# Transformer layer with dense MoE on Trainium2: causal-mask multiplies from GpSimd to VectorE, and the gate block from before attention to after it

## The chip, the cores and the metric

The kernel runs on the 8 NeuronCores of one Trainium2 chip (two dies of four cores). Every core runs the same program on its own batch element; nothing is exchanged between them. The metric is the device time in microseconds of the slowest core. The engines are named as in the profile: PE (TensorE matmul), PEld (its weight loads), DVE (VectorE), ACT (ScalarE), POOL (GpSimd), SP (SyncE, which here only issues DMAs).

## The reference

For each of 8 batch elements, x has 2048 rows of 1024 values.

```python
xn = layernorm(x)
x = x + attn(xn, w_qkv, w_out) + ffn(xn, w1, b1, w2, b2, wr, br)

def attn(x, w_qkv, w_out):            # 16 heads of 64, causal
    q, k, v = split(x @ w_qkv.T)
    scores = where(causal, (q @ k.T) / 8, -1e30)
    return (softmax(scores) @ v) @ w_out.T

def ffn(x, w1, b1, w2, b2, wr, br):   # 4 experts, hidden 4096, top 2
    topv, topi = top_k(x @ wr + br, 2)
    gates = softmax(topv)
    y = gelu(x @ w1[e] + b1[e]) @ w2[e] + b2[e]      # for every expert e
    c = gelu(b1[e]) @ w2[e] + b2[e]
    return sum over k of gates_k * (y[topi_k] - c[topi_k] + sum_e c[e])
```

## The kernel before

The program is written as blocks. Within a block each engine has its own list of instructions in the order of the Python code and meets the others only through semaphores; at the end of a block all engines meet at a barrier (the rows of the profile that name L43 or L47, as releaser `PEq L43`).

1. Block 1 and 2: constants (the causal mask tile `masks`, 128x2048 bf16, is made on POOL, L236), layer norm, transposes of the normalised x into `xn_fm`, router logits `lgt`, their top-2 mask `mask2`, and the projections to `q_fm`, `k_fm` and `v_ext`.
2. Block 3: SP issues eight DMA transposes of `w_out` (L565). Then comes the **gate block**, L569 to L599: 16 small exponentials on ACT (`exa`, L571), a multiply, 16 reductions, a reciprocal and 16 scalings on DVE that give `agate` (the gate of each row and expert, L575 to L585), and 16 PE transposes (L593) with a DVE copy each (L596) into `aem`. `agate` is first read by the feed-forward (L913, L918) and `aem` by its last bias matmuls (L1023). Then attention.
3. Block 4: the dense feed-forward, 16 slabs of weights (4 experts by 4 groups of 1024 hidden units) by 4 tiles of 512 rows: `emit_h` (L868, gelu L876) and `emit_y` (L899, accumulate L918).
4. Block 5: x, the attention result (through the DRAM buffer `attn_sc`) and the accumulator are added and stored.

**Attention.** The queries come in four quarters `qt` of 512 columns. Quarter qt has `npair` = 2(qt+1) steps p, each over two key blocks of 128. For each quarter a loop goes over eight head pairs (h0, h1), and within it over p. For each head and step: two score matmuls (`emit_pair`, L691 and L697, into the PSUM pair P45 or P67), one exponential of 128x1024 on ACT (L705) into `p_sb`, and two AV matmuls (`emit_av`, L726 and L733) into one of three PSUM slots. There is one `p_sb` for h0 and one for h1. The last two steps of every head cross the diagonal, and there `p_sb` is multiplied in place by `masks` (L713): 4 masks for each head pair, 4 x 32 = 128 in all. In quarter 0 every step is such a step; in quarter 3 two of eight are.

PE's order within a head pair is QK h0, QK h1, then for each p: AV h0, QK h0 of p+1, AV h1, QK h1 of p+1. A finished head is normalised late: DVE copies its row of sums (`rrow`, L647, `flush_stage1`, at the end of its head pair), then within the next head pair `flush_stage2` takes Ln and Exp on ACT (L655, L658), spreads the result with a one-row matmul (L664), copies it on DVE (`rbsb`, L668) and multiplies on DVE into `attn_cat` (L676), which frees the slot. The output projection of a quarter (`emit_opuser`, L760, L765, with a DVE copy L773 and a store L780) is interleaved into the first head pair of the next quarter; that of quarter 3 stands at the end of the block. In quarter 3 POOL also issues loads of feed-forward weights: w1 of slab 0 in two halves behind the second and fourth head pair (L819, L825), and w2 of slab 0 and both weights of slab 1 behind the last AV matmul (L616, L608).

The mask and what it hangs on, before:

```python
W("gpsimd", "SS", ve)
vm = I("gpsimd", "SG", lambda g, psb=psb, j=j: g.tensor_tensor(
    psb[:], psb[:], masks[:, j * 1024:(j + 1) * 1024], ALU.mult))
v_use[p] = vm
v_uses[p] = "SG"
```

Of the kernel before, what the change touches and what calls it, by code (L numbers as in the profile page):

```python
# [18 lines left out]
NTS = 16  # L19
# [30 lines left out]
def build_nc():  # L50
# [41 lines left out]
    lgt = at("lgt", [128, 64], F32, 2976)  # L92
# [80 lines left out]
    TRS = [P4, P5, P6, P7]  # L173
# [8 lines left out]
    def W(eng, s, v):  # L182
        if v > 0:
            P.emit(eng, lambda e, s=s, v=v: e.wait_ge(sem[s], v))  # L184

    def Wtr(eng, entry):
        if isinstance(entry, tuple):
            for k in range(0, len(entry), 2):
                W(eng, entry[k], entry[k + 1])
        else:  # L190
            W(eng, "SV", entry)

    def I(eng, s, fn, n=1):
# [175 lines left out]
    tr_idx = 0  # L369
    tr_evac = {}  # L370
# [55 lines left out]
    for q_ in range(4):  # L426
        for k_ in range(4):
            ts = q_ * 4 + k_
# [6 lines left out]
            if ts >= 2:  # L435
# [37 lines left out]
        trp = TRS[tr_idx % 4]  # L473
# [17 lines left out]
        for k_ in range(4):  # L491
            ts = q_ * 4 + k_
            trp = TRS[tr_idx % 4]
            W("tensor", "SV", v_lem)
            if tr_idx >= 4:
                Wtr("tensor", tr_evac[tr_idx - 4])
            v_t = I("tensor", "ST", lambda t, k_=k_, trp=trp: t.transpose(
                trp[0:128, 0:4], lgt_em[0:4, k_ * 128:(k_ + 1) * 128],
                ident[0:4, 0:4]))
# [66 lines left out]
            bass.AP(w_outT, fc * 128, [[8192, 128], [1024, 8], [1, 128]]),  # L566
            woutbf_h.ap()[fc * 128:(fc + 1) * 128, :]), 16)

    v_ex_last = 0  # L569
    for ts in range(NTS):  # L570
        v_ex_last = I("scalar", "SS", lambda s, ts=ts: s.activation(  # L571
            exa[:, ts * 4:(ts + 1) * 4], lgt[:, ts * 4:(ts + 1) * 4], AF.Exp,
            bias=nm1a[:, ts:ts + 1]))
    W("vector", "SS", v_ex_last)
    E("vector", lambda v: v.tensor_tensor(g2a[:], exa[:], mask2[:], ALU.mult))  # L575
    E("vector", lambda v: v.drain())
    for ts in range(NTS):
        E("vector", lambda v, ts=ts: v.tensor_reduce(
            Sa[:, ts:ts + 1], g2a[:, ts * 4:(ts + 1) * 4], AX.X, ALU.add))
    E("vector", lambda v: v.drain())  # L580
    E("vector", lambda v: v.reciprocal(rSa[:], Sa[:]))
    E("vector", lambda v: v.drain())
    v_ag = [0] * NTS
    for ts in range(NTS):
        v_ag[ts] = I("vector", "SV", lambda v, ts=ts: v.tensor_scalar_mul(  # L585
            agate[:, ts * 4:(ts + 1) * 4], g2a[:, ts * 4:(ts + 1) * 4],
            rSa[:, ts:ts + 1]))
    for ts in range(NTS):
        trp = TRS[tr_idx % 4]
        if tr_idx >= 4:  # L590
            Wtr("tensor", tr_evac[tr_idx - 4])
        W("tensor", "SV", v_ag[ts])
        v_t = I("tensor", "ST", lambda t, ts=ts, trp=trp: t.transpose(  # L593
            trp[0:4, 0:128], agate[:, ts * 4:(ts + 1) * 4], ident[:]))
        W("vector", "ST", v_t)
        v_ev = I("vector", "SV", lambda v, ts=ts, trp=trp: v.tensor_copy(  # L596
            aem[:, ts * 128:(ts + 1) * 128], trp[0:4, 0:128]))
        tr_evac[tr_idx] = v_ev
        tr_idx += 1  # L599

    w1g = [w1g0, w1g1]
    w2g = [w2g0, w2g1]
    h_sb = [h_sb0, h_sb1]
# [30 lines left out]
    sc_guard = [("SV", tr_evac[tr_idx - 1]), ("SV", tr_evac[tr_idx - 1])]  # L634
# [47 lines left out]
    def emit_pair(qt, head, p, npair, v_use, v_uses):  # L682
        bpar = head % 2
        pair = head // 2
        hr = (head % 2) * 64
        pb = PB[bpar]
        psb = p_sb[bpar]
        kb0 = 2 * p
        gs, gv = sc_guard[bpar]
        W("tensor", gs, gv)  # L690
        E("tensor", lambda t, kb0=kb0, pb=pb, hr=hr, pair=pair, qt=qt: t.matmul(  # L691
            pb[:, 0:512],
            k_fm[hr:hr + 64, pair * 2048 + kb0 * 128:pair * 2048 + (kb0 + 1) * 128],
            q_fm[hr:hr + 64, pair * 2048 + qt * 512:pair * 2048 + (qt + 1) * 512],
            start=True, stop=True))
# [12 lines left out]
        v_use[p] = ve
        v_uses[p] = "SS"
        if p >= npair - 2:  # L710
            j = p - (npair - 2)
            W("gpsimd", "SS", ve)
            vm = I("gpsimd", "SG", lambda g, psb=psb, j=j: g.tensor_tensor(  # L713
                psb[:], psb[:], masks[:, j * 1024:(j + 1) * 1024], ALU.mult))
            v_use[p] = vm
            v_uses[p] = "SG"

    def emit_av(qt, head, p, npair, v_use, v_uses, v_avp):
        bpar = head % 2
# [64 lines left out]
    for qt in range(4):  # L784
# [3 lines left out]
        for i_hp, hp in enumerate(hporder):  # L788
# [247 lines left out]
    v_ag = [0] * 4  # L1036
# [66 lines left out]
```

How the kernel before makes its waits and increments, by code:

```python
    def W(eng, s, v):  # L182
        if v > 0:
            P.emit(eng, lambda e, s=s, v=v: e.wait_ge(sem[s], v))
# [8 lines left out]
    def I(eng, s, fn, n=1):  # L193
        if n >= 16 and C[s] > 0:
            W(eng, s, C[s])
        C[s] += n
        v = C[s]
        P.emit(eng, lambda e, fn=fn, s=s, n=n: fn(e).then_inc(sem[s], n))
        return v
```

## Time and profile before

| what | value |
|---|---|
| median of the 2 runs shown | 3450.77 us (3350.36 and 3551.18) |
| the profiled execution's own time | 3365.17 us |
| its span on the slowest core | 3363.6 us (the eight cores: 3335.6 to 3363.6) |
| PE busy | 2832.9 us, 84% |
| DVE, ACT, POOL busy | 697.5, 863.9 and 305.3 us |
| attention, first score matmul to feed-forward's first matmul | 377.5 to 1361.0 us |

The span runs from the first to the last instruction of one core; what lies around it is 1.6 us here. A row of the timeline gives start, duration, engine, line, operation and, in brackets, how long the engine had been idle and what released it. The granted PE clock (PEclk) is a share of 2.4 GHz: 0.50 is 1.2 GHz.

### The profile page before, as it was taken

To read this page: it belongs to the slowest core of one execution; us is meant where nothing else is said; L and a number is where in the kernel's file an instruction comes from. 1 tells how busy PE (TensorE), PEld (TensorE's weight loads), DVE (VectorE), ACT (ScalarE), POOL (GpSimd) and SP (SyncE) were. 2 spreads that over 40 slices of the span, in tenths; PEclk is the share of its full clock that TensorE was granted. 3 is DMA by queue.
4 is the path that set the end of the run, shared out by engine and by line. 5 is a ranking of instruction groups with operands and counts; after the bars stand their busy time and mean duration, and the time that the engine had idled before them with its cause. 6 is when DMAs were issued, how large, how long until landed. Compare 5 with 4: busy or idle time off the path is not lost. (4 is left out here: it accounts for less than half of the span.)

```text
span 3363.6 us, 29884 instructions; the slowest of 8 cores (3335.6 to 3363.6 us)
## 1 busy us (share of the span) xinstructions
PE 2832.9 (84%) x10932; PEld 1085.4 (32%) x11124; DVE 697.5 (21%) x929; ACT 863.9 (26%) x1169; POOL 305.3 (9%) x189
## 2 busy tenths in 40 slices
PE   3679657667777876899999999999999999999970
PEld 1234201111111111344444444444444444444420
DVE  5441321111111001011111111111111111111224
ACT  2212244434444553211111111121111111111100
POOL 0000352322212221000000000000000000000000
PEclk9779656565555556899999999999999999999955
DMA  6710100000001004121331133023303330330017
GB/s 148 96 33 1 25 0 25 0 25 0 0 13 25 13 0 74 27 33 18 50 51 23 29 51 50 12 39 51 51 1 50 51 46 5 51 50 1 1 53 246
DMA packets 79709, 127.86 MB, mean 38 GB/s; under 512 B 36174, under 2 KB 36302, under 8 KB 79314
## 3 DMA queue, kind: packets, MB, share of 16 engines
q0 software_dynamic: 33616, 75.50, 15.1%
q1 hardware_dynamic: 45954, 50.44, 4.9%
q8 instruction: 96, 1.57, 0.2%
q14 instruction: 43, 0.35, 0.0%
HBM read 176.26 MB, written 25.17 MB: 60 GB/s over the span
## 5 line engine op out<-in xcount | busy, mean ns | idle before, releaser
L868 PE MATMUL P<-xn_fm,w1g 128*128 128x512 bf16 x4024 | 891.5, 380 | 32.0 <-PEq L43 27.4
L899 PE MATMUL P<-w2g,h_sb 128*128 128x512 bf16 x4001 | 889.3, 379 | 5.0
L876 ACT ACTIVATE h_sb<-P,b_sb 128x512 bf16<-128x512 f32 x512 | 351.9, 687 | 1445.2 <-PE P L868 1445.2
L918 DVE SCALAR_TENSOR_TENSOR accum<-P,agate,accum 128x1024 f32<-128x1024 f32 x240 | 308.2, 1284 | 1379.8 <-PE P L899 1379.8
L868 PEld LDWEIGHTS P<-xn_fm,w1g 128*128 128x128 bf16 x4096 | 400.0, 98 | 515.7 <-issue 37.4
L899 PEld LDWEIGHTS P<-w2g,h_sb 128*128 128x128 bf16 x4096 | 400.8, 98 | 483.2
L705 ACT ACTIVATE p_sb<-P,cneg 128x1024 bf16<-128x1024 f32 x320 | 353.2, 1114 | 488.8 <-PE P L697 488.5
L726 PE MATMUL P<-p_sb,v_ext 128*65 128x512 bf16 x320 | 192.1, 600 | 211.8 <-POOL p_sb L713 152.5
L713 POOL TENSOR_TENSOR p_sb<-p_sb,masks 128x1024 bf16<-128x1024 bf16 x128 | 268.8, 2117 | 896.2 <-ACT p_sb L705 896.0
L733 PE MATMUL P<-p_sb,v_ext 128*65 128x512 bf16 x320 | 195.6, 611 | 0.0
L726 PEld LDWEIGHTS P<-p_sb,v_ext 128*65 128x65 bf16 x320 | 41.2, 129 | 470.8 <-issue 469.5
L668 DVE COPY rbsb<-P 64x512 f32<-64x512 f32 x64 | 43.7, 683 | 669.2 <-PE P L664 668.9
L697 PE MATMUL P<-q_fm,k_fm 64*128 64x512 bf16 x320 | 176.5, 612 | 0.0
L691 PE MATMUL P<-q_fm,k_fm 64*128 64x512 bf16 x320 | 169.2, 586 | 7.2 <-DVE proj L773 6.5
L608 POOL DMA_DIRECT2D w1g<-w x15 | 13.2, 877 | 1640.2 <-PE P L941 1640.2
L285 PE MATMUL P<-xn_fm,wqkvT 128*128 128x512 bf16 x436 | 125.2, 432 | 23.9 <-DVE k_fm L304 18.9
L691 PEld LDWEIGHTS P<-q_fm,k_fm 64*128 64x128 bf16 x320 | 28.9, 99 | 209.6 <-issue 209.6
L446 PE MATMUL P<-ident,xnf 128*128 128x128 f32 x128 | 33.8, 404 | 57.8 <-ACT xnf L437 55.6
L664 PE MATMUL P<-rbr,ones_bf 1*64 1x512 bf16 x64 | 39.5, 616 | 45.0 <-ACT rbr L658 40.8
L285 PEld LDWEIGHTS P<-xn_fm,wqkvT 128*128 128x128 bf16 x448 | 47.8, 108 | 90.1 <-issue 77.1
L760 PE MATMUL P<-w_outT,attn_cat 128*128 128x512 bf16 x232 | 61.2, 419 | 11.2 <-ACT p_sb L705 7.9
L941 PE MATMUL P<-w2g,hfake 128*1 128x512 bf16 x256 | 57.8, 379 | 0.0
(113 smaller groups left out, 989.2 us busy)
## 6 DMA issues: line engine op xcount, KB each, us to landing
w2g<-w POOLq DMA_DIRECT2D x16, 2048.0 KB, 29.4
w1g<-w POOLq DMA_DIRECT2D x15, 2048.0 KB, 18.5
attn_sc<-proj SPq DMA_DIRECT2D x16, 512.0 KB, 2.6
xrg<-x SPq DMA_DIRECT2D x4, 2048.0 KB, 11.7
arg<-attn_sc SPq DMA_DIRECT2D x4, 2048.0 KB, 16.7
y<-outr SPq DMA_DIRECT2D x16, 512.0 KB, 2.6
xA<-x SPq DMA_DIRECT2D x3, 2048.0 KB, 38.2
wqkv_bf<-w_qkv POOLq DMA_DIRECT2D x3, 2048.0 KB, 24.4
```

The lines of the kernel that those rows point to most:

```text
L285: t.matmul(pt[:, off:off + 512], wqkvT[:, dc * 3072 + fc8 * 128:dc * 3072 + (fc8 + 1) * 128], xn_fm[:, dc * 2048 + tt * 512:dc * 2048 + (t ...
L691: E("tensor", lambda t, kb0=kb0, pb=pb, hr=hr, pair=pair, qt=qt: t.matmul(pb[:, 0:512], k_fm[hr:hr + 64, pair * 2048 + kb0 * 128:pair * 20 ...
L697: t.matmul(pb[:, 512:1024], k_fm[hr:hr + 64, pair * 2048 + (kb0 + 1) * 128:pair * 2048 + (kb0 + 2) * 128], q_fm[hr:hr + 64, pair * 2048 + ...
L705: ve = I("scalar", "SS", lambda s, pb=pb, psb=psb: s.activation(psb[:], pb[:, 0:1024], AF.Exp, bias=cneg8[:, 0:1]))
L713: vm = I("gpsimd", "SG", lambda g, psb=psb, j=j: g.tensor_tensor(psb[:], psb[:], masks[:, j * 1024:(j + 1) * 1024], ALU.mult))
L726: E("tensor", lambda t, p=p, head=head, psb=psb, sl=sl: t.matmul(sl[0:65, :], bass.AP(v_ext, 2 * p * VW + head * 65, [[NTS * VW, 128], [1, ...
L733: psb=psb, sl=sl, av_stop=av_stop: t.matmul(sl[0:65, :], bass.AP(v_ext, (2 * p + 1) * VW + head * 65, [[NTS * VW, 128], [1, 65]]), psb[:, ...
L760: t.matmul(pb[:, half * 512:(half + 1) * 512], ac[:, ec * 512 + ts4 * 128:ec * 512 + (ts4 + 1) * 128], w_outT[:, ec * 1024 + half * 512:ec ...
L868: t.matmul(PH67[par][:, 0:512], w1g[buf][:, dc * 1024 + hc * 128:dc * 1024 + (hc + 1) * 128], xn_fm[:, dc * 2048 + tt * 512:dc * 2048 + (t ...
L876: s.activation(h_sb[tt % 2][:, hc * 512:(hc + 1) * 512], PH67[par][:, 0:512], AF.Gelu, bias=b1_sb[:, e_ * 32 + g_ * 8 + hc:e_ * 32 + g_ * ...
L899: pt=pt, st=st, sp=sp: t.matmul(pt[:, half * 512:(half + 1) * 512], h_sb[tt % 2][:, hc * 512 + ts4 * 128:hc * 512 + (ts4 + 1) * 128], w2g[ ...
L918: v.scalar_tensor_tensor(accum[:, tsg * 1024:(tsg + 1) * 1024], pt[:, 0:1024], agate[:, tsg * 4 + e_:tsg * 4 + e_ + 1], accum[:, tsg * 102 ...
```

## The change

Two edits.

1. The mask multiply of `emit_pair` is issued on DVE in place of POOL, with the same operands, and signals DVE's semaphore SV, on which the AV matmul then waits.
2. The gate block is emitted after the whole attention loop, at the end of the same block. Before its transposes PE waits for the last two projection copies, which use the same PSUM tiles.

```diff
-    v_ex_last = 0
-    for ts in range(NTS):
-        v_ex_last = I("scalar", "SS", lambda s, ts=ts: s.activation(
...
@@ emit_pair
         if p >= npair - 2:
             j = p - (npair - 2)
-            W("gpsimd", "SS", ve)
-            vm = I("gpsimd", "SG", lambda g, psb=psb, j=j: g.tensor_tensor(
+            W("vector", "SS", ve)
+            vm = I("vector", "SV", lambda v, psb=psb, j=j: v.tensor_tensor(
                 psb[:], psb[:], masks[:, j * 1024:(j + 1) * 1024], ALU.mult))
             v_use[p] = vm
-            v_uses[p] = "SG"
+            v_uses[p] = "SV"
@@ after the loop over qt, ahead of P.brk()
+    v_ex_last = 0
+    for ts in range(NTS):
+        v_ex_last = I("scalar", "SS", lambda s, ts=ts: s.activation(
...
+    W("tensor", *sc_guard[0])
+    W("tensor", *sc_guard[1])
+    for ts in range(NTS):
+        trp = TRS[tr_idx % 4]
...
```

PE where attention's block begins, before: the last gate transposes, then the first score matmuls and the first AV, which waits for POOL's semaphore SG.

```order
L593 MATMUL P45<-ident_43,agate_76 4x128 [waits SV] x2
L593 MATMUL P67<-ident_43,agate_76 4x128 [waits SV] x2
L691 MATMUL P45<-q_fm_90,k_fm_91 128x512 [waits SV]
L697 MATMUL P45<-q_fm_90,k_fm_91 128x512
L691 MATMUL P67<-q_fm_90,k_fm_91 128x512 [waits SV]
L697 MATMUL P67<-q_fm_90,k_fm_91 128x512
L726 MATMUL P23<-p_sb0_118,v_ext_92 65x512 [waits SG]
L733 MATMUL P23<-p_sb0_118,v_ext_92 65x512
```

The same place after the change: the barrier, then the score matmuls at once, and the AV waits for DVE's semaphore SV.

```order
L47 UNCONDITIONAL_BRANCH [waits barrier_Pool_Activation_PE_DVE_SP_release]
L659 MATMUL P45<-q_fm_90,k_fm_91 128x512 [waits SV]
L665 MATMUL P45<-q_fm_90,k_fm_91 128x512
L659 MATMUL P67<-q_fm_90,k_fm_91 128x512 [waits SV]
L665 MATMUL P67<-q_fm_90,k_fm_91 128x512
L694 MATMUL P23<-p_sb0_118,v_ext_92 65x512 [waits SV]
L701 MATMUL P23<-p_sb0_118,v_ext_92 65x512
L659 MATMUL P45<-q_fm_90,k_fm_91 128x512 [waits SS]
L665 MATMUL P45<-q_fm_90,k_fm_91 128x512
```

The 16 transposes are gone from here, and nothing else stands between the barrier and the score matmuls.

DVE in quarter 0, before, from the end of the first head pair on (`rrow` are the copies of the sums, `rbsb` and `attn_cat` the late normalisation of the previous head pair):

```order
L647 COPY rrow0_120<-P23 1x512 [waits ST]
L647 COPY rrow1_121<-P23 1x512 [waits ST]
L668 COPY rbsb0_126<-P01 64x512 [waits ST]
L676 TENSOR_TENSOR attn_cat_116<-P23,rbsb0_126 64x512
L668 COPY rbsb1_127<-P01 64x512 [waits ST]
L676 TENSOR_TENSOR attn_cat_116<-P23,rbsb1_127 64x512
L647 COPY rrow0_120<-P01 1x512 [waits ST]
L647 COPY rrow1_121<-P23 1x512 [waits ST]
```

DVE at the same place after the change:

```order
L615 COPY rrow0_120<-P23 1x512 [waits ST]
L615 COPY rrow1_121<-P23 1x512 [waits ST]
L681 TENSOR_TENSOR p_sb0_118<-p_sb0_118,masks_78 128x1024 [waits SS]
L681 TENSOR_TENSOR p_sb1_119<-p_sb1_119,masks_78 128x1024 [waits SS]
L636 COPY rbsb0_126<-P01 64x512 [waits ST]
L644 TENSOR_TENSOR attn_cat_116<-P23,rbsb0_126 64x512
L681 TENSOR_TENSOR p_sb0_118<-p_sb0_118,masks_78 128x1024 [waits SS]
L681 TENSOR_TENSOR p_sb1_119<-p_sb1_119,masks_78 128x1024 [waits SS]
L636 COPY rbsb1_127<-P01 64x512 [waits ST]
L644 TENSOR_TENSOR attn_cat_116<-P23,rbsb1_127 64x512
L615 COPY rrow0_120<-P01 1x512 [waits ST]
L615 COPY rrow1_121<-P23 1x512 [waits ST]
```

The masks of a head pair's first step now stand behind the two `rrow` copies of the head pair before it, and those of its second step behind the normalisation of that pair's first head.

PE at the end of attention's block, before: the last projection matmuls, the barrier, the feed-forward's first matmuls.

```order
L760 MATMUL P67<-w_outT_84,attn_cat2_117 128x512 [waits SQW,SV]
L760 MATMUL P67<-w_outT_84,attn_cat2_117 128x512 x14
L765 MATMUL P67<-w_outT_84,attn_cat2_117 128x512
L43 UNCONDITIONAL_BRANCH
L47 UNCONDITIONAL_BRANCH [waits barrier_Pool_Activation_PE_DVE_SP_release]
L868 MATMUL P67<-xn_fm_83,w1g0_103 128x512 [waits SW0]
```

After the change:

```order
L728 MATMUL P67<-w_outT_84,attn_cat2_117 128x512 x14
L733 MATMUL P67<-w_outT_84,attn_cat2_117 128x512
L837 MATMUL P45<-ident_43,agate_76 4x128 [waits SV] x2
L837 MATMUL P67<-ident_43,agate_76 4x128 [waits SV] x2
L837 MATMUL P45<-ident_43,agate_76 4x128 [waits SV] x2
L837 MATMUL P67<-ident_43,agate_76 4x128 [waits SV] x2
L837 MATMUL P45<-ident_43,agate_76 4x128 [waits SV] x2
L837 MATMUL P67<-ident_43,agate_76 4x128 [waits SV] x2
L837 MATMUL P45<-ident_43,agate_76 4x128 [waits SV] x2
L837 MATMUL P67<-ident_43,agate_76 4x128 [waits SV] x2
L43 UNCONDITIONAL_BRANCH
L47 UNCONDITIONAL_BRANCH [waits barrier_Pool_Activation_PE_DVE_SP_release]
L870 MATMUL P67<-xn_fm_83,w1g0_103 128x512 [waits SW0]
```

The transposes now stand between the last projection matmul and the barrier; DVE's and ACT's gate instructions likewise stand last in their lists ahead of it.

## Rows read from the trace of the kernel before

**Rows 1.** Groups by line: name, shapes, xcount | busy us, mean ns | idle before, releaser.
```profile
L713 POOL TENSOR_TENSOR p_sb<-p_sb,masks 128x1024 bf16<-128x1024 bf16 x128 | 268.8, 2117 | 896.2 <-ACT p_sb L705 896.0
...
L726 PE MATMUL P<-p_sb,v_ext 128*65 128x512 bf16 x320 | 192.1, 600 | 211.8 <-POOL p_sb L713 152.5 <-DVE rrow L647 27.5 <-DVE attn_cat L676 22.3
```

**Rows 2.** Windows, steady unmasked attention: us, busy by engine, PEclk, DMA share, GB/s.
```profile
1280.00:1290.00 10.00, 10.00 (x22) 1.56 (x20) 0.00 (x0) 5.81 (x6) 0.00 (x0) 0.50 0.00 0
```

**Rows 3.** Timeline where attention's block starts: start us, us, engine, line, operation.
```profile
364.84 1.28 ACT L571 ACT_TABLE_LOAD   x1 [55.55 <-PEq L43]
...
366.13 3.11 ACT L571 ACTIVATE exa<-lgt,nm1a 128x4 f32<-128x4 f32 x16
...
377.51 0.71 PE L691 MATMUL P<-q_fm,k_fm 64*128 64x512 bf16 x2 [0.53 <-DVE aem L596]
...
378.61 2.12 ACT L705 ACTIVATE p_sb<-P,cneg 128x1024 bf16<-128x1024 f32 x2 [9.37 <-PE P L697]
```

**Rows 4.** Groups by line: table load behind a wait; two VectorE tensor_tensor forms.
```profile
L676 DVE TENSOR_TENSOR attn_cat<-P,rbsb 64x512 bf16<-64x512 f32 x64 | 43.8, 684 | 8.5 <-issue 5.0 <-PE P L697 0.5
...
L392 DVE TENSOR_TENSOR xsq<-xA 128x1024 f32<-128x1024 f32 x16 | 19.6, 1225 | 7.6 <-DMA xA<-x 6.4
...
L413 ACT ACT_TABLE_LOAD x1 | 1.3, 1283 | 16.2 <-DVE var_a L410 16.2
```

**Rows 5.** Timeline, one head pair of query quarter 3, from score matmul to score matmul.
```profile
1190.84 0.61 PE L691 MATMUL P<-q_fm,k_fm 64*128 64x512 bf16 x2
...
1218.94 4.19 POOL L713 TENSOR_TENSOR p_sb<-p_sb,masks 128x1024 bf16<-128x1024 bf16 x2 [29.78 <-ACT p_sb L705]
...
1221.20 0.61 PE L726 MATMUL P<-p_sb,v_ext 128*65 128x512 bf16 x1 [1.72 <-POOL p_sb L713]
...
1223.28 0.60 PE L726 MATMUL P<-p_sb,v_ext 128*65 128x512 bf16 x1
...
1226.87 0.61 PE L726 MATMUL P<-p_sb,v_ext 128*65 128x512 bf16 x1 [1.60 <-POOL p_sb L713]
...
1228.94 0.60 PE L726 MATMUL P<-p_sb,v_ext 128*65 128x512 bf16 x1 [1.04 <-POOL p_sb L713]
...
1230.47 0.61 PE L691 MATMUL P<-q_fm,k_fm 64*128 64x512 bf16 x2
```

**Rows 6.** Timeline, one head pair of query quarter 0.
```profile
406.06 0.61 PE L691 MATMUL P<-q_fm,k_fm 64*128 64x512 bf16 x2
...
407.24 2.12 ACT L705 ACTIVATE p_sb<-P,cneg 128x1024 bf16<-128x1024 f32 x2 [3.81 <-PE P L697]
407.72 1.29 DVE L647 COPY rrow<-P 1x512 f32<-1x512 f32 x2
...
410.86 0.61 PE L726 MATMUL P<-p_sb,v_ext 128*65 128x512 bf16 x1 [3.77 <-POOL p_sb L713]
...
414.17 0.61 PE L726 MATMUL P<-p_sb,v_ext 128*65 128x512 bf16 x1 [0.75 <-DVE attn_cat L676]
...
417.09 0.61 PE L726 MATMUL P<-p_sb,v_ext 128*65 128x512 bf16 x1 [0.93 <-POOL p_sb L713]
...
419.84 0.61 PE L726 MATMUL P<-p_sb,v_ext 128*65 128x512 bf16 x1 [1.71 <-POOL p_sb L713]
...
421.36 0.61 PE L691 MATMUL P<-q_fm,k_fm 64*128 64x512 bf16 x2
```

**Rows 7.** Timeline, first head pair of quarter 1, where the output projection is interleaved.
```profile
531.28 0.38 PE L726 MATMUL P<-p_sb,v_ext 128*65 128x512 bf16 x1 [0.31 <-POOL p_sb L713]
```

**Rows 8.** Timeline from the last attention load issue to the feed-forward's first matmul.
```profile
1310.17 0.95 POOL L616 DMA_DIRECT2D w2g<-w  x1 [1.72 <-PE P L733]
...
1337.11 1.22 DVE L773 COPY proj<-P 128x1024 f32<-128x1024 f32 x1 [1.81 <-DMA attn_sc<-proj]
...
1361.00 29.99 PE L868 MATMUL P<-xn_fm,w1g 128*128 128x512 bf16 x126 [27.39 <-PEq L43]
```

**Rows 9.** Windows just before the feed-forward starts.
```profile
1355.00:1360.00 5.00, 0.00 (x0) 0.00 (x0) 0.00 (x0) 0.00 (x0) 0.00 (x0) 0.50 0.96 167
```

More of the change, by code:

```diff
@@ L567, in build_nc @@
             woutbf_h.ap()[fc * 128:(fc + 1) * 128, :]), 16)
-    v_ex_last = 0
-    for ts in range(NTS):
-        v_ex_last = I("scalar", "SS", lambda s, ts=ts: s.activation(
[L572 to L599, printed above, removed]
     w1g = [w1g0, w1g1]
@@ L841, in build_nc @@
             op_defer = []
+    v_ex_last = 0
+    for ts in range(NTS):
+        v_ex_last = I("scalar", "SS", lambda s, ts=ts: s.activation(
+            exa[:, ts * 4:(ts + 1) * 4], lgt[:, ts * 4:(ts + 1) * 4], AF.Exp,
+            bias=nm1a[:, ts:ts + 1]))
+    W("vector", "SS", v_ex_last)
+    E("vector", lambda v: v.tensor_tensor(g2a[:], exa[:], mask2[:], ALU.mult))
+    E("vector", lambda v: v.drain())
+    for ts in range(NTS):
+        E("vector", lambda v, ts=ts: v.tensor_reduce(
+            Sa[:, ts:ts + 1], g2a[:, ts * 4:(ts + 1) * 4], AX.X, ALU.add))
+    E("vector", lambda v: v.drain())
+    E("vector", lambda v: v.reciprocal(rSa[:], Sa[:]))
+    E("vector", lambda v: v.drain())
+    v_ag = [0] * NTS
+    for ts in range(NTS):
+        v_ag[ts] = I("vector", "SV", lambda v, ts=ts: v.tensor_scalar_mul(
+            agate[:, ts * 4:(ts + 1) * 4], g2a[:, ts * 4:(ts + 1) * 4],
+            rSa[:, ts:ts + 1]))
+    W("tensor", *sc_guard[0])
+    W("tensor", *sc_guard[1])
+    for ts in range(NTS):
+        trp = TRS[tr_idx % 4]
+        if tr_idx >= 4:
+            Wtr("tensor", tr_evac[tr_idx - 4])
+        W("tensor", "SV", v_ag[ts])
+        v_t = I("tensor", "ST", lambda t, ts=ts, trp=trp: t.transpose(
+            trp[0:4, 0:128], agate[:, ts * 4:(ts + 1) * 4], ident[:]))
+        W("vector", "ST", v_t)
+        v_ev = I("vector", "SV", lambda v, ts=ts, trp=trp: v.tensor_copy(
+            aem[:, ts * 128:(ts + 1) * 128], trp[0:4, 0:128]))
+        tr_evac[tr_idx] = v_ev
+        tr_idx += 1
     P.brk()
```

## The prediction, made before the changed kernel ran

> **What bounds the kernel now.** I read the groups by line first, for what PE waits for. The AV matmul L726 sat idle 211.8 us, 152.5 of them until POOL's mask L713 had ended; the mask takes 2117 ns and runs 128 times [rows 1]. The windows show that between masks PE is the bound: from 1280 to 1290 us it is busy 10.00 of 10 us, ACT 5.81, and the granted clock is 0.50, 1.2 GHz [rows 2]. So attention is PE's time plus its waits, and of the waits the masks make up the most. The timeline at the block's start gives the other part that the change touches: between the barrier (364.84) and the first score matmul (377.51) PE has nothing but the gate block [rows 3]. Last I read the block's end, since that is where the gate block goes: DVE's last copy ends at 1338.3 and PE starts the feed-forward only at 1361.0, after 27.39 us of idle time at the barrier, while the DMA engines are 0.96 busy until 1360 [rows 8, 9].
>
> **Edit 2, the start.** The first score matmul moves from 377.51 to about the barrier's 364.84, 12.7 us earlier. One thing is given back. ACT's table load of 1.28 us ran beside the barrier ahead of the gate's exponentials; now the first instruction on ACT is attention's exponential, which waits for the scores. The load at L413 started only when the wait of its instruction had ended [rows 4], so I take the whole 1.28 us as uncovered (the other bound is 0). That leaves 11.4 us (11.4 to 12.7). The eight w_out transposes on SP are issued at the barrier in either kernel and are first needed far later.
>
> **Edit 2, the end.** ACT, long idle by then, has its 16 exponentials (3.11 us) done before DVE's last copy ends. From the end of those exponentials to the first score matmul the gate chain took 377.51 - 369.24 = 8.3 us [rows 3], so it ends near 1338.3 + 8.3 = 1346.6, counted in times of before. What the feed-forward waits for is the barrier, and I read the barrier as waiting for the three weight loads whose issue begins on POOL at 1310.17, right behind the last AV matmul: the DMA engines go quiet at 1360, and PE starts 1 us later. From issue to PE's start that is 50.8 us, a stretch that moves as a whole with the last AV matmul. The gate chain lies inside it with 14 us to spare: cost 0 (bounds 0 and 8.3 plus some issue, if the cover is not there).
>
> **Edit 1, what a mask costs on DVE.** No row shows a bf16 multiply from SBUF on DVE. The rows on either side are 684 ns for a tensor_tensor of 512 f32 columns and 1225 ns for one of 1024 f32 columns [rows 4]. By columns the mask would be like the second, by bytes per partition like the first, since 1024 bf16 are as many bytes as 512 f32. I take 0.69 us, by bytes, and keep 1.225 as a rival.
>
> The Trainium skill (VectorE: DVE Perf Modes, the perf-mode tier table) says that tensor_tensor on packed bf16 operands in SBUF yields two results a cycle where f32 yields one, and its walkthrough gives 1224 ns for 2048 columns; an estimate from its fixed part of some 150 cycles is 690 ns for 1024. No row here shows the rule for bf16; its f32 half agrees with the 1225 ns. By it the sum below stands; without it the sum would be that of the first rival.
>
> **A head pair of quarters 1 to 3.** It takes 1230.47 - 1190.84 = 39.6 us in quarter 3 [rows 5]. Four AV matmuls follow masks. (a) The first comes at 1221.20 after 1.72 us of waiting; its mask began at 1218.94. On DVE that mask ends at 1219.63 and, with the 0.14 us that POOL's end took to reach PE (1218.94 + 2.12 to 1221.20), PE goes on at 1219.77: a wait of 0.3 remains, 1.43 saved. (b) The second comes at 1223.28, 0.15 after POOL's two masks end (1218.94 + 4.19); four matmuls from 1221.20 on keep PE until 1223.1 (22 take 10 us [rows 2], a little more where AV and score matmuls alternate), so 0.15 is saved. (c) The third waits 1.60 and keeps 0.3: 1.30 saved. (d) The fourth waits 1.04. Its scores are issued just before the third AV: 1.18 us from first score matmul to exponential (406.06 to 407.24 [rows 6]), 1.11 for it, 0.15 to the mask, 0.69 for the mask and 0.14 back make 3.27 us, against 1.93 us of matmuls and the 0.3 of (c). So 1.04 remains and nothing is saved: here the wait for the mask turns into one for the exponential. Sum 2.87 us for a head pair. In these quarters DVE's other work lies at the start of a head pair (normalisation) and behind its last AV (sum copies), so no other instruction stands in front of a mask for long.
>
> There are 24 such head pairs. In the first of quarter 1 the output projection lies between the masks and the AV that need them (one wait of 0.31 is left there [rows 7]), so I count nothing for it, and half for the first of quarter 2: 22.5 x 2.87 = 64.6 us.
>
> **A head pair of quarter 0.** It takes 421.36 - 406.06 = 15.3 us [rows 6]. The first exponential ends at 407.24 + 1.11 = 408.35, but DVE is at the two sum copies until 409.01, and the mask now stands behind them: it runs from 409.05 to 409.75, and the AV comes at 409.9 in place of 410.86, 0.95 saved. The second AV (414.17) waits for attn_cat, not for a mask, and moves along. The third loses its wait of 0.93 whole, for the mask starts beside the scores of the other head. The fourth waits 1.71 now and, by (d)'s chain with no wait in (c)'s place, keeps 3.27 - 1.93 = 1.34: 0.37 saved. Sum 2.25 us, times 8 = 18.0 us. Queued behind a waiting mask on DVE stand the next rbsb copy and the multiply into attn_cat; both wait for a matmul that PE issues later than the masked scores, so they lose nothing.
>
> **Sum.** 11.4 + 64.6 + 18.0 = 94.0 us. The profiled execution took 3365.2 us by its own time (span 3363.6): 3365.2 - 94.0 = 3271. The median shown for before, 3450.8, is of two runs 200 us apart; the lower of them, 3350.4, lies 15 us under the profiled time and would give 3256.
>
> **Rivals.**
> *The mask runs at the f32 rate, 1.225 us.* Waits (a) and (c) keep 0.84 each in place of 0.30, (b) still goes and (d) stays, so 1.79 us is saved for a head pair, 22.5 x 1.79 = 40.3. In quarter 0 the first wait saves 0.42 (0.95 less 0.53), the third still about 0.9 and the fourth loses 0.16: 1.2 x 8 = 9.6. With 11.4 that is 61.3: 3304. For it: the only 1024-column row is 1225 ns. Against: half the bytes.
> *The end has no cover.* If the barrier's 22 us after DVE's last copy were its own and not the loads', the gate chain would add its 8.3 us: 3280. Against: the DMA engines' 0.96 right up to 1360 [rows 9].
> *The clock rises.* With the stalls gone PE might be granted 1.0 in attention. ACT would then bound the steps at 5.81 of 10 us [rows 2]. 160 steps less the 64 masked ones are 96, of 8 matmuls each and about 3.6 us (22 matmuls in 10 us): 349 x 0.42 = 147 us more, 3124. Against: the window has PE busy throughout and the clock is 0.50 all the same.
> The Trainium skill (TensorE: Matmul & The Clock Gate, What's actually happening) has activity release the full clock and idleness take it back. By that rule alone this rival would win; the trace disagrees, with 0.50 at 10.00 us busy in 10.
> *Slower: DVE's masks become slower than POOL's.* DVE, unlike POOL, also has copies in its list, and one engine holding both could make a mask's turn effectively 2.45 us, twice the f32 row. Then waits (a), (b) and (c) each grow by 2.45 - 2.12 = 0.33, 1.0 us a head pair; in quarter 0, with 0.55 to 0.8 behind the sum copies, about 1.8. 22.5 + 14.4 - 11.4 = 25.5 us slower, 3391. It decides from about 2.2 us a mask on, and from 2.9 us the kernel is over 2% slower. For it: the two sum copies in front of quarter 0's masks. Against: both VectorE rows are far below, and in the later quarters no copy stands in front of a mask.
> *The change does not do what it says*, the wait only moving to the exponential: that is so for (d), and is in the sum.
>
> **How the numbers follow.** Forecast 0.76, f32 rate 0.12, no cover 0.06, clock 0.02, slower 0.04. About 2% is what a measurement of this kernel can tell from no change, 67 us, so below 3298. The forecast, the uncovered end and the clock are faster, but of the forecast I set 0.05 aside for gains that turn out a third smaller; of the f32-rate case, which lies on the line, a quarter counts as faster: 0.71 + 0.06 + 0.02 + 0.03 = 0.82. Within 2%: 0.05 + 0.09 + a quarter of the slower case, 0.15 in all after rounding; slower by over 2%, the rest: 0.03. The range goes from 3235 (the lower run of before less 94 is 3256, and less 21 for a mask shorter than any row and for errors of my chain) to 3330 (the f32 rate, 3304, with an uncovered end 8.3 more, and the 15 us between the two low times on top). It leaves out the clock and the slower case.
>
> **What would show it.** In the profile after: L681 on DVE, 128 times at about 0.69 us; PE's wait for it near 0.3 us for the first and third masked AV and 1.0 for the fourth, 50 to 70 us in all against 152.5; a head pair of quarter 3 at 36.7 us and one of quarter 0 at 13.0; the first score matmul right behind the barrier; the gate chain ended more than 10 us before the feed-forward's first matmul, which still comes some 51 us after POOL's L584 issue. The prediction is wrong if a mask takes over 1.1 us, if the head pairs keep their 39.6 us because another wait fills in, or if the barrier moves with the gate chain.

## The result, and the profile after

| | before | after |
|---|---|---|
| ratio, after to before, with its 95% interval | | 0.9708 (0.9668 to 0.9747) |
| profiled execution's own time | 3365.17 us | 3266.81 us |
| median of all executions | 3637.33 us (10) | 3361.26 us (11) |
| lowest execution | 3350.36 us | 3261.92 us |

The two medians hold executions in which one die was granted a lower clock, and can't be compared; the ratio is of undisturbed executions alone. It means 2.9% faster, 98 us of 3365. The prediction had 94 us (3271 of 3365, 0.972). Its range of 3235 to 3330 us holds the profiled execution and misses the median of all eleven, 3361.26. A twelfth execution of the kernel after, 3245.37 us, is on record and not counted in that median.

Where the time went, from the first and last starts of four lines (the V projection L324; the first score matmul of a step, L691 before and L659 after; the AV matmul L726 before and L694 after; the feed-forward's L868 before and L870 after), each the median over the eight cores:

| stretch | before, us | after, us |
|---|---|---|
| end of V projection to first score matmul | 14.1 | 1.6 |
| first score matmul to last AV | 933.1 | 840.8 |
| last AV to feed-forward's first matmul | 51.1 | 51.4 |
| feed-forward, first to last start of L868 / L870 | 1797.2 | 1797.4 |

So 12.5 us go at the start and 92.3 us in attention, only 0.3 us comes back at the end, and the feed-forward is untouched: 104.5 us on a typical core.

The groups by line of the kernel after, to set beside [rows 1]:

```profile
L694 PE MATMUL P<-p_sb,v_ext 128*65 128x512 bf16 x320 | 191.1, 597 | 124.1 <-DVE p_sb L681 66.3 <-DVE rrow L615 26.0 <-DVE attn_cat L644 22.2
...
L681 DVE TENSOR_TENSOR p_sb<-p_sb,masks 128x1024 bf16<-128x1024 bf16 x128 | 88.0, 691 | 408.2 <-ACT p_sb L673 408.2
```

The mask takes 691 ns on DVE in place of 2117 ns on POOL, and PE's wait for it fell from 152.5 to 66.3 us. The waits for `rrow` and `attn_cat` are what they were (27.5 and 22.3 before).

The timeline of a head pair's masked end in quarter 3, beside [rows 5]:

```profile
1061.22 0.69 DVE L681 TENSOR_TENSOR p_sb<-p_sb,masks 128x1024 bf16<-128x1024 bf16 x1 [21.10 <-ACT p_sb L673]
...
1062.06 0.61 PE L694 MATMUL P<-p_sb,v_ext 128*65 128x512 bf16 x1 [0.26 <-DVE p_sb L681]
...
1064.01 0.61 PE L694 MATMUL P<-p_sb,v_ext 128*65 128x512 bf16 x1
...
1066.27 0.61 PE L694 MATMUL P<-p_sb,v_ext 128*65 128x512 bf16 x1 [0.25 <-DVE p_sb L681]
...
1067.38 0.69 DVE L681 TENSOR_TENSOR p_sb<-p_sb,masks 128x1024 bf16<-128x1024 bf16 x1 [1.26 <-ACT p_sb L673]
...
1068.22 0.61 PE L694 MATMUL P<-p_sb,v_ext 128*65 128x512 bf16 x1 [0.92 <-DVE p_sb L681]
...
1069.75 0.61 PE L659 MATMUL P<-q_fm,k_fm 64*128 64x512 bf16 x2
```

The first masked AV waits 0.26 us (1.72 before), the second nothing, the third 0.25 (1.60), the fourth 0.92 (1.04). DVE had been idle 21.10 us ahead of the first mask.

The timeline of a head pair of quarter 0, beside [rows 6]:

```profile
396.76 0.61 PE L659 MATMUL P<-q_fm,k_fm 64*128 64x512 bf16 x2
...
398.43 1.29 DVE L615 COPY rrow<-P 1x512 f32<-1x512 f32 x2
399.65 1.27 DVE L681 TENSOR_TENSOR p_sb<-p_sb,masks 128x1024 bf16<-128x1024 bf16 x2
...
400.57 0.61 PE L694 MATMUL P<-p_sb,v_ext 128*65 128x512 bf16 x1 [2.77 <-DVE p_sb L681]
...
403.88 0.61 PE L694 MATMUL P<-p_sb,v_ext 128*65 128x512 bf16 x1 [0.75 <-DVE attn_cat L644]
...
405.80 0.64 PE L694 MATMUL P<-p_sb,v_ext 128*65 128x512 bf16 x1
...
408.08 0.60 PE L694 MATMUL P<-p_sb,v_ext 128*65 128x512 bf16 x1 [1.21 <-DVE p_sb L681]
...
409.61 0.61 PE L659 MATMUL P<-q_fm,k_fm 64*128 64x512 bf16 x2
```

The first mask starts at 399.65, where DVE's two sum copies end (398.43 + 1.29 = 399.72, within 0.07 us); the AV follows at 400.57. Score matmul to score matmul it is 12.85 us (15.3 before).

The timeline where attention's block begins, beside [rows 3]:

```profile
372.84 0.50 PE L659 MATMUL P<-q_fm,k_fm 64*128 64x512 bf16 x2 [1.27 <-PEq L43]
...
373.51 1.28 ACT L673 ACT_TABLE_LOAD   x1 [64.58 <-PE P L665]
374.80 2.12 ACT L673 ACTIVATE p_sb<-P,cneg 128x1024 bf16<-128x1024 f32 x2
```

Scores run right behind the barrier. The table load came after the scores, as taken from L413, with its whole 1.28 us; the exponential follows it at once. But the scores were shorter: the load starts 0.67 us behind the first score matmul, where the exponential of before started after 1.10 us. The granted clock was still 1.00 here (from 372.8 to 374.0 us) and 0.50 at the same place before. So the first exponential starts 1.96 us behind the first score matmul (1.10 before), and 0.86 us is given back.

The timeline at the block's end, beside [rows 8]:

```profile
1216.51 0.88 POOL L584 DMA_DIRECT2D w2g<-w  x1 [145.31 <-PE P L701]
...
1221.61 3.10 ACT L813 ACTIVATE exa<-lgt,nm1a 128x4 f32<-128x4 f32 x16
...
1243.37 1.22 DVE L741 COPY proj<-P 128x1024 f32<-128x1024 f32 x1 [1.53 <-DMA attn_sc<-proj]
1244.51 0.22 DVE L817 TENSOR_TENSOR g2a<-exa,mask 128x64 f32<-128x64 f32 x1
...
1249.58 3.10 DVE L840 COPY aem<-P 4x128 f32<-4x128 f32 x12 [0.29 <-PE P L837]
...
1266.49 18.75 PE L870 MATMUL P<-xn_fm,w1g 128*128 128x512 bf16 x74 [14.19 <-PEq L43]
```

The gate chain ends at 1252.7 (1249.58 + 3.10), 13.8 us ahead of the feed-forward, which starts 50.0 us behind the issue of the first of POOL's three loads (50.8 before).

### The profile page after: what moved, and what is told of

Read it like the earlier page. It is cut to its first block and busy times, and to the rows that moved or that the text cites. A ratio compares the mean times of both kernels' runs of the same rounds, so it can differ in the third digit from the quotient of the medians.

```text
span 3265.3 us, 30078 instructions; the slowest of 8 cores (3230.9 to 3265.3 us)
## 1 busy us (share of the span) xinstructions
PE 2852.7 (87%) x11124; PEld 1088.2 (33%) x11124; DVE 784.8 (24%) x1057; ACT 863.5 (26%) x1169; POOL 36.2 (1%) x61
## 3 DMA queue, kind: packets, MB, share of 16 engines
q0 software_dynamic: 33616, 75.50, 14.9%
## 5 line engine op out<-in xcount | busy, mean ns | idle before, releaser
L870 PE MATMUL P<-xn_fm,w1g 128*128 128x512 bf16 x4096 | 897.1, 380 | 14.2 <-PEq L43 14.2
L870 PEld LDWEIGHTS P<-xn_fm,w1g 128*128 128x128 bf16 x4096 | 400.1, 98 | 502.5 <-issue 24.6
L694 PE MATMUL P<-p_sb,v_ext 128*65 128x512 bf16 x320 | 191.1, 597 | 124.1 <-DVE p_sb L681 66.3
L681 DVE TENSOR_TENSOR p_sb<-p_sb,masks 128x1024 bf16<-128x1024 bf16 x128 | 88.0, 691 | 408.2 <-ACT p_sb L673 408.2
L659 PE MATMUL P<-q_fm,k_fm 64*128 64x512 bf16 x320 | 168.3, 582 | 7.9 <-DVE proj L741 6.5
L694 PEld LDWEIGHTS P<-p_sb,v_ext 128*65 128x65 bf16 x320 | 41.0, 128 | 379.0 <-issue 377.6
L659 PEld LDWEIGHTS P<-q_fm,k_fm 64*128 64x128 bf16 x320 | 28.9, 99 | 209.1 <-issue 209.1
L728 PE MATMUL P<-w_outT,attn_cat 128*128 128x512 bf16 x240 | 66.3, 438 | 9.6 <-ACT p_sb L673 7.9
L319 PE MATMUL P<-wqkvT,xn_fm 128*128 128x512 bf16 x224 | 61.0, 418 | 0.0
## 6 DMA issues: line engine op xcount, KB each, us to landing
arg<-attn_sc SPq DMA_DIRECT2D x4, 2048.0 KB, 14.4
xA<-x SPq DMA_DIRECT2D x3, 2048.0 KB, 38.1
```

Source lines behind the costliest of these rows:

```text
L681: vm = I("vector", "SV", lambda v, psb=psb, j=j: v.tensor_tensor(psb[:], psb[:], masks[:, j * 1024:(j + 1) * 1024], ALU.mult))
L694: E("tensor", lambda t, p=p, head=head, psb=psb, sl=sl: t.matmul(sl[0:65, :], bass.AP(v_ext, 2 * p * VW + head * 65, [[NTS * VW, 128], [1, ...
L728: t.matmul(pb[:, half * 512:(half + 1) * 512], ac[:, ec * 512 + ts4 * 128:ec * 512 + (ts4 + 1) * 128], w_outT[:, ec * 1024 + half * 512:ec ...
L870: t.matmul(PH67[par][:, 0:512], w1g[buf][:, dc * 1024 + hc * 128:dc * 1024 + (hc + 1) * 128], xn_fm[:, dc * 2048 + tt * 512:dc * 2048 + (t ...
```

## The experiments

### The mask alone

```diff
# the kernel before, with only
-            W("gpsimd", "SS", ve)
-            vm = I("gpsimd", "SG", lambda g, psb=psb, j=j: g.tensor_tensor(
+            W("vector", "SS", ve)
+            vm = I("vector", "SV", lambda v, psb=psb, j=j: v.tensor_tensor(
```

> The mask on VectorE alone; the gate block stays ahead of attention. If the two edits add up as in the prediction, this keeps 83 to 87 us of the gain (ratio to before 0.974 to 0.975), the wait of L726 for the mask is near 66 us as in the changed kernel, and the score matmuls again start 12.6 us behind the barrier. Rival: the edits are worth different shares (the gate block's move is the larger one, ratio above 0.98).

Measured: ratio 0.9724 (0.9705 to 0.9744). Groups by line of this kernel:

```profile
L726 PE MATMUL P<-p_sb,v_ext 128*65 128x512 bf16 x320 | 191.3, 598 | 123.2 <-DVE p_sb L713 65.7 <-DVE rrow L647 26.2 <-DVE attn_cat L676 21.9
...
L713 DVE TENSOR_TENSOR p_sb<-p_sb,masks 128x1024 bf16<-128x1024 bf16 x128 | 87.9, 690 | 407.5 <-ACT p_sb L705 407.5
```

By the same four lines: 14.1 us from the V projection to the first score matmul, as before, and 840.1 us of attention, as after. So the whole attention gain, 93.0 us, is the mask's. It is 6 to 10 us more than expected; which head pairs it comes from stands in the section on why the prediction was right or wrong.

### The gate block's move alone

```diff
# the changed kernel, with the mask back on GpSimd
-            W("vector", "SS", ve)
-            vm = I("vector", "SV", lambda v, psb=psb, j=j: v.tensor_tensor(
+            W("gpsimd", "SS", ve)
+            vm = I("gpsimd", "SG", lambda g, psb=psb, j=j: g.tensor_tensor(
```

> The gate block's move alone; the mask stays on GpSimd. Expected 11 to 12.7 us under before (ratio 0.996 to 0.997), with the L726 wait for the mask still 152 us and the feed-forward starting 51 to 52 us behind the last AV matmul, as before. Rival (the end has no cover): the gate chain's 8 to 13 us come back there and the ratio is 1.000.

Measured: ratio 0.9945 (0.9902 to 0.9988). The interval holds the expected 0.996 to 0.997 and ends just short of the rival's 1.000. Groups by line:

```profile
L694 PE MATMUL P<-p_sb,v_ext 128*65 128x512 bf16 x320 | 192.2, 601 | 212.6 <-POOL p_sb L681 153.4 <-DVE rrow L615 26.0 <-DVE attn_cat L644 21.9
```

The stretches say it more sharply: 1.7 us in place of 14.1 at the start, attention 932.4 (933.1 before), last AV to feed-forward 51.1. The move is worth 12.4 us, and it costs nothing at the end. The stretches of the two runs add: 12.4 + 92.8 (983.8 before and 891.0 with the mask alone, from first score to feed-forward) is 105.2, against 104.4 for both edits (14.1 + 983.8 less 1.6 + 891.9).

### Every mask twice

```diff
             W("vector", "SS", ve)
+            E("vector", lambda v, psb=psb, j=j: v.tensor_tensor(
+                psb[:], psb[:], masks[:, j * 1024:(j + 1) * 1024], ALU.mult))
+            E("vector", lambda v: v.drain())
             vm = I("vector", "SV", lambda v, psb=psb, j=j: v.tensor_tensor(
```

> Every mask is applied twice in a row on VectorE (the values are 0 and 1, so nothing changes in the output); a mask is then worth 1.4 us. By the chains of the prediction waits (a) and (c) grow by the 0.7 us each, (b) and (d) stay, so a head pair of quarter 3 goes from 36.5 to 37.9 us and one of quarter 0 from 12.9 to 14.3, about 41 us in all: 57 us under before, ratio 0.983. Rival: the mask is hidden by exponentials anyway and the second one costs nothing, ratio 0.971; or all four masked AV matmuls wait, 4 x 0.7 x 32 = 90 us, ratio 0.998.

Measured: ratio 0.9794 (0.9721 to 0.9868). It holds the expected 0.983 and leaves out both rivals, the nearer (0.971) by 0.001 alone. The stretch says it more clearly: attention took 888.5 us, 47.7 more than after (expected 41; the rivals 0 and 90). Timeline of the masked end of a head pair in quarter 3:

```profile
1094.39 0.69 DVE L681 TENSOR_TENSOR p_sb<-p_sb,masks 128x1024 bf16<-128x1024 bf16 x1 [21.10 <-ACT p_sb L673]
...
1095.16 0.69 DVE L684 TENSOR_TENSOR p_sb<-p_sb,masks 128x1024 bf16<-128x1024 bf16 x1
...
1096.00 0.61 PE L697 MATMUL P<-p_sb,v_ext 128*65 128x512 bf16 x1 [1.02 <-DVE p_sb L684]
...
1097.95 0.61 PE L697 MATMUL P<-p_sb,v_ext 128*65 128x512 bf16 x1
...
1100.97 0.60 PE L697 MATMUL P<-p_sb,v_ext 128*65 128x512 bf16 x1 [1.02 <-DVE p_sb L684]
...
1102.92 0.61 PE L697 MATMUL P<-p_sb,v_ext 128*65 128x512 bf16 x1 [0.92 <-DVE p_sb L684]
```

The first and third wait grew from 0.26 and 0.25 to 1.02 us, by the second mask's 0.77; the second still does not wait, and the fourth stayed at 0.92. A head pair of quarter 3 took 38.1 us and one of quarter 0 14.4, as the chains had it (37.9 and 14.3). What a mask costs is therefore twice its length for a head pair, not four times and not nothing: 36.6 to 38.1 us in quarter 3 and 12.85 to 14.4 in quarter 0.

The run also suggests that it hardly matters which engine does the mask, only how long it takes. At two lengths for each of 32 head pairs, 64 us of attention for each us of mask, one goes from the doubled mask (0.77 + 0.69 = 1.46 us on DVE, 888.5 us of attention) to the mask of before (2.12 us on POOL) with 42 us more, 931: an estimate from these rows, against 933.1 measured.

### No mask

```diff
-        if p >= npair - 2:
-            j = p - (npair - 2)
-            W("vector", "SS", ve)
-            vm = I("vector", "SV", lambda v, psb=psb, j=j: v.tensor_tensor(
...
```

This kernel leaves the causal mask out of the computation.

> The changed kernel with the causal mask left out of the computation: AV waits for the exponential alone. By the chains, waits (a) and (c) go (0.25 each) and (d), 0.92 us, keeps what the exponential alone makes, 0.92 - 0.84 = 0.1: a head pair of quarter 3 at 35.1 to 35.7 us, 25 to 35 us less than the changed kernel in all. If instead (d) is a wait for the exponential, as the prediction put it, it stays near 0.9 with another name, and the head pair is at 36.0.

Measured: attention 815.2 us, 25.6 less than after, at the lower edge of what was expected; a head pair of quarter 3 took 35.8 us, between the expected 35.1 to 35.7 and the rival's 36.0. The timeline of a head pair's end:

```profile
1042.50 0.63 PE L687 MATMUL P<-p_sb,v_ext 128*65 128x512 bf16 x1
...
1043.98 0.61 PE L687 MATMUL P<-p_sb,v_ext 128*65 128x512 bf16 x1 [0.42 <-ACT p_sb L673]
...
1045.28 0.60 PE L632 MATMUL P<-rbr,ones_bf 1*64 1x512 bf16 x1 [0.27 <-ACT rbr L626]
```

The fourth AV now waits 0.42 us for the exponential alone (0.1 was expected, 0.9 by the rival), and right behind it PE waits 0.27 us for `rbr`, a chain of Ln and Exp on ACT that had been hidden by the longer wait. So of the fourth wait's 0.92 us 0.50 goes with the mask and 0.42 stays with the exponential: the prediction, which called it a wait for the exponential, was half right. What the mask on DVE still costs in all is 25.6 us.

### The loads of slab 1 behind the barrier

```diff
             W("gpsimd", "ST", pending[1][4])
             emit_w2_dma(0)
-            emit_w1_dma(1)
-            emit_w2_dma(1)
...
     W("vector", "SP1", C["SP1"])
+    emit_w1_dma(1)
+    emit_w2_dma(1)
```

> The changed kernel with the weight loads of slab 1 (w1 and w2) issued by GpSimd right behind the barrier and not ahead of it; only slab 0's w2 stays in front. If the barrier waits for the loads, the feed-forward's first matmul comes as soon as the gate chain and the one load have ended, 14 to 17 us earlier than in the changed kernel (35 to 38 us behind the last AV matmul in place of 51.5), ratio to before 0.966 to 0.967. Rival: the barrier's time is its own or VectorE's; then the first matmul stays 51 us behind the last AV, ratio 0.971. Slab 1 is needed 112 us into the feed-forward, so its later load should cost nothing.

Measured: ratio 0.9705 (0.9587 to 0.9823), no verdict on 15 us. From the last AV to the feed-forward it is 36.5 us in place of 51.4; attention (840.9) is unchanged, and so is the feed-forward on the median core (1796.5). Timeline:

```profile
1190.97 0.88 POOL L584 DMA_DIRECT2D w2g<-w  x1 [145.30 <-PE P L701]
...
1216.08 1.23 DVE L741 COPY proj<-P 128x1024 f32<-128x1024 f32 x1 [2.23 <-PE P L733]
...
1221.81 3.20 PE L835 MATMUL P<-ident,agate 128*4 128x128 f32 x12 [1.34 <-DVE aem L838]
...
1225.86 34.02 PE L870 MATMUL P<-xn_fm,w1g 128*128 128x512 bf16 x128 [0.85 <-PEq L43]
1226.10 0.87 POOL L576 DMA_DIRECT2D w1g<-w  x1 [34.24 <-POOLq L43]
```

The barrier did wait for the loads: with two of the three behind it, it opens 14.9 us earlier. PE had ended the gate transposes (L835) only 0.85 us earlier, so the barrier now opens with the end of the gate chain, and the next run, which takes that chain away, opens it earlier still. In the kernel after, the block's end was free for the gates only because these loads were in front of the barrier.

### The gates out of the end, with late loads

```diff
# the gate block's exponentials and VectorE part behind the sixth head pair of quarter 3,
# its transposes between the last AV and the output projection
+            if qt == 3 and i_hp == 5:
+                gates_ag = emit_gates()
...
+        if qt == 3:
+            emit_gate_tr(0, 8, gates_ag)
         flush_stage2(pending[0])
+        if qt == 3:
+            v_gt = emit_gate_tr(8, 16, gates_ag)
```

> The kernel with late loads, and the gate block taken out of the end: its exponentials and VectorE part go behind the sixth head pair of quarter 3, where VectorE is idle for 21 us, and its 16 transposes go between the last AV matmul and the output projection, where PE waits 6.8 us for the last normalisations. With the loads late the barrier opens when the gate chain has ended (36.5 us behind the last AV matmul), so this should bring it to 27 to 31 us; if one load of w2 is what the barrier waits for there, it stays at 33 or more. Ratio to before 0.962 to 0.966.

Measured: 3224.98 us for the profiled execution, and no ratio. Last AV to feed-forward is 31.3 us, just outside the expected 27 to 31, and 5.2 less than with the gates at the end. Attention took 842.1 us, 1.2 more than with late loads: it is lost in the head pair behind which the gates' VectorE part was put (38.2 us in place of 36.9). Timeline:

```profile
1202.72 6.07 PE L728 MATMUL P<-w_outT,attn_cat 128*128 128x512 bf16 x15 [1.78 <-DVE attn_cat L644]
...
1219.54 1.22 DVE L741 COPY proj<-P 128x1024 f32<-128x1024 f32 x1 [2.23 <-PE P L733]
...
1221.77 18.47 PE L885 MATMUL P<-xn_fm,w1g 128*128 128x512 bf16 x77 [2.41 <-PEq L43]
```

The feed-forward's first matmul now comes 1.0 us behind the last projection copy (1219.54 + 1.22 = 1220.76). The transposes did not fit wholly into PE's waits: the output projection starts 12.3 us behind the last AV (1190.46), where with late loads alone it started 9.6 us behind it (1189.39 to 1199.02).

### Fewer columns in the masked steps

```diff
+        c = 256 if p == npair - 1 else 0          # scores and exponential from column c on
-            pb[:, 0:512],
+            pb[:, c:512],
...
+        ca = 256 if p == npair - 1 else 0         # AV, first and second key block
+        cb = 384 if p == npair - 1 else 128 if p == npair - 2 else 0
-            sl[0:65, :],
+            sl[0:65, ca:512],
...
-                psb[:], psb[:], masks[:, j * 1024:(j + 1) * 1024], ALU.mult))
+                bass.AP(psb, j * 256, [[1024, 128], [640, 2], [1, 128]]),
...
```

> The changed kernel, where in the two masked steps of a head the columns that the causal mask makes zero are mostly not computed: 512 columns of scores, 512 of the exponential and 768 of AV less for each head and quarter, and the mask multiplies only the two diagonal blocks of 128 columns. If attention is bound by PE's columns at 1.2 GHz, 1280 columns are 1.07 us and 64 heads (16 in each of 4 quarters) make 68 us, and waits (a) and (c) go too: first score to last AV at 765 to 785 us in place of 841, ratio to before 0.948 to 0.956. Rival: the chain of scores, exponential, mask and AV bounds the masked steps; then only the shorter exponential and mask count, some 0.8 us a head pair, and it stays above 810 us.

Measured: ratio 0.9507 (0.9471 to 0.9543); attention 785.0 us, 55.8 less than after, at the upper end of what was expected. Groups by line:

```profile
L706 PE MATMUL P<-p_sb,v_ext 128*65 128x512 bf16 x256 | 154.3, 603 | 89.3 <-DVE p_sb L688 28.2 <-DVE rrow L615 26.1 <-DVE attn_cat L644 25.3
...
L688 DVE TENSOR_TENSOR p_sb<-p_sb,masks 128x256 bf16<-128x256 bf16 x128 | 37.2, 291 | 403.1 <-ACT p_sb L675 332.5 <-ACT p_sb L678 70.6
...
L706 PE MATMUL P<-p_sb,v_ext 128*65 128x256 bf16 x64 | 25.3, 397 | 28.9 <-DVE p_sb L688 28.9
```

A head pair of quarter 3 took 34.7 us (36.6). The rival, above 810 us, falls. PE's columns, 68 us by the estimate in the expectation, are enough for the gain; the waits that were to go with them did not: PE's waits for the mask are 28.2 + 28.9 = 57.1 us in all (66.3 after), and its wait for `rbr` grew from 42.0 to 55.8 us. That the chain of scores, exponential and mask is late again because PE has less work beside it is likely, and no run shows it by itself.

### Both together

```diff
# fewer columns, late loads, gates out of the end: the three edits above
```

> Both together: first score to last AV as in the run with fewer columns, and 27 to 31 us from the last AV to the feed-forward. The two do not share a wait, so the gains should add: ratio to before 0.940 to 0.950.

Measured: ratio 0.9440 (0.9405 to 0.9475). Attention took 786.2 us and last AV to feed-forward 30.2 us, each within 1.2 us of its part (785.0 and 31.3). The gains add, and the kernel beats both others.

## Why the prediction was right or wrong

**The start** (11.4 us). Right in size: 12.5 us shorter to the first score matmul and 0.86 given back make 11.6. The table load itself cost its whole 1.28 us, as the prediction took it; 0.4 us came from the first scores, which ran at a granted clock of 1.00 in place of 0.50, and that the prediction did not have.

**The mask's duration** (0.69 us, by bytes). Right: 691 ns. The f32-rate rival falls, and with it the slower case; the Trainium skill's rule (VectorE: DVE Perf Modes, the perf-mode tier table), that bf16 operands in SBUF double tensor_tensor's rate, is what this row shows: 1024 columns in 691 ns where f32 took 1225.

**A head pair of quarters 1 to 3** (2.87 us). It was 3.05: 39.64 to 36.59. Waits (a) and (c) came out at 0.26 and 0.25 (0.30 in the chain), (d) at 0.92 (1.04). The step that called (d) a wait for the exponential was half right, as the run without masks showed. That masks count in (a) and (c) alone held when they were doubled.

**The first head pairs of quarters 1 to 3** (0, half and one gain). From score to score, median over the eight cores, they went from 31.1 to 31.05, 43.3 to 40.9 and 51.8 to 46.3: gains of 0, 2.5 and 5.5 in place of 0, 1.4 and 2.9. (On the two profiled cores it was -0.9, 1.3 and 4.7; these three vary from core to core, the others hardly.) Here the prediction missed that the clock moves. Windows over the first two head pairs of quarter 3 (the columns are those of [rows 2]; the granted clock is the third figure from the end), before:

```profile
980.80:1032.20 51.40, 38.15 (x127) 11.28 (x128) 7.01 (x8) 17.66 (x16) 8.42 (x4) 0.80 0.10 41
1032.20:1071.90 39.70, 31.78 (x69) 5.15 (x69) 2.05 (x3) 20.18 (x20) 8.38 (x4) 0.50 0.00 1
```

and after:

```profile
913.60:960.30 46.70, 36.86 (x129) 11.30 (x128) 9.71 (x12) 17.66 (x16) 0.00 (x0) 0.86 0.11 45
960.30:996.50 36.20, 30.85 (x67) 5.09 (x66) 4.90 (x8) 20.17 (x20) 0.00 (x0) 0.56 0.00 0
```

The granted clock is above 0.50 in both kernels while the output projection is interleaved, and its stretch at 1.00 lasted 30.7 us in the first two head pairs of quarter 3 before and 37.5 us after. With the mask on VectorE alone it was 37.5 us too, and with every mask twice, where this head pair gained only 2.2 us, 30.7. That the 6.8 us more at the full clock are a part of the gain fits these runs; no run changed the clock by itself.

**Quarter 0** (2.25 us a head pair). It was 2.45 (15.3 to 12.85). The masks behind the two sum copies cost what was said.

**The end** (0). Right (0.3 us), and by the cause named: the barrier waits for the loads, as the run with late loads showed. The rival without cover falls.

**The sum** (94.0 us). On a typical core it was 104.5. Attention gave 92.3 where the terms make 82.6: quarter 0 gave 19.4 (18.0), the three first head pairs 8.0 (4.3), the other 21 some 64 (60.3). The execution's time gave 98.4, nearer to the forecast by luck. The slowest core of either kernel was late ahead of everything the change touches, and the one of the kernel after by 7.8 us more: its V projection ended at 371.2 us (core 1; 343.8 to 348.5 on cores 2 to 7), that of before at 363.4 (core 6; 343.1 to 348.0 on cores 0 to 5).

**The clock.** The rival with a clock of 1.00 throughout attention falls: in steady unmasked steps the granted clock stayed at 0.50 with PE busy 10.00 us in 10, before [rows 2] and after (1080 to 1090 us). But the prediction's picture, 0.50 all through attention, was not right either: before, 81.9 us between the first score matmul and the last AV ran at 1.00, all of them about the output projections, and after, 91.0 us on the median core. The Trainium skill (TensorE: Matmul & The Clock Gate, What's actually happening) says that activity releases the full clock; PE's busy share alone does not sort these stretches, for from 1000 to 1020 us of before, at 0.99, PE was busy only 16.83 us of 20.

**The range** was wrong. It ran from 3235 to 3330, and the median of the eleven executions is 3361.26. The step that failed is the one under "Sum" that set aside the median shown for before, 3450.8 from two executions 200 us apart, and took the profiled execution as the only base; the range then allowed 15 us for the spread between executions. What the runs showed in its place is a spread of 391 us: of the eleven executions after, five lie between 3262 and 3275 us and six between 3361 and 3653, and the ten of before run from 3350 to 3782. The other base would have been no better founded. 3450.8 less 94 is 3357, close to 3361.26, but by luck: the ten executions of before have their median at 3637.33, and that less 94 is 3543. The change in time was right to 4.4 us (98.4 for 94.0) and the repeated terms within 0.2 us a head pair; the absolute time of a median was not.

## What to carry to other kernels

A mask or other elementwise step in a chain of scores, exponential and AV costs its length only where the chain is later than PE's own work in between; count the masked steps one by one (here two of four were hidden). Look at the granted clock over the whole of a stage, not in one window: here it rose from 0.50 to 1.00 where the output projection was interleaved. Work moved to a block's end is free only while something else holds the barrier, and the next change (here the loads moved behind it) can take that cover away. Where two runs of one kernel lie 6% apart, forecast the ratio, and let the range of an absolute time reach both.

## What the runs showed of the hardware that was not expected

A granted clock of 0.81, which is neither 1.2 nor 2.4 GHz. In the windows from 320 to 340 us, inside the projections, the slowest core of the kernel after had:

```profile
320.00:340.00 20.00, 20.00 (x77) 8.26 (x76) 6.45 (x20) 0.00 (x0) 0.00 (x0) 0.81 0.00 1
```

and the profiled core of the kernel before:

```profile
320.00:340.00 20.00, 19.89 (x92) 9.11 (x93) 7.94 (x22) 0.00 (x0) 0.00 (x0) 1.00 0.00 1
```

At 0.81 PE is as busy as at 1.00 and has 77 matmuls in 20 us in place of 92. By core the same window of the kernel after shows 0.81 on cores 0 and 1 and 1.00 on the six others, and it is by this that the slowest core was late into attention. It is no mark of the changed kernel. The profiled core of before had 0.81 too, only earlier:

```profile
225.00:295.00 70.00, 67.93 (x257) 28.74 (x264) 11.58 (x63) 16.17 (x24) 0.00 (x0) 0.81 0.00 1
```

There cores 6 and 7 had it and the others 1.00 (326 matmuls on core 1 in the same 70 us). With late loads cores 6 and 7 had 0.81 for 161.5 us from 1233 us on, at the feed-forward's beginning, where cores 0 to 3 had 1.00, and their feed-forward took 1825 us in place of 1796.5. The Trainium skill (TensorE: Matmul & The Clock Gate, Seeing it yourself) has a limiter to 13/16, 81%, that takes a whole die once three of its cores run dense matmuls. The value agrees; the rest does not: here all eight cores run them, most at 1.00, and in these traces it was two cores of a die that fell, while the other two did not. Only with fewer columns did all four cores of a die show 0.81, for 4 to 5 us each at about 1156 us.
